# Attention on one core: halves of two key tiles weighed in pairs, and maxima moved within their turns

## The reference, cut to what matters

```python
h = gn(x)                                    # 32 groups of 16 channels
q, k, v = Wq h, Wk h, Wv h                   # 8 heads of 64 channels
attn = softmax(q^T k over the 2304 keys)     # no scaling
out  = x + gamma * (attn v) + Wsc h
```

## Time and profile before

| what | value |
| --- | --- |
| median of 3 runs | 3061.2 us (3058.46 to 3061.65) |
| time of the profiled execution | 3061.98 us |
| its span, first to last instruction | 3060.3 us |
| TensorE busy | 2967.9 us (97%) |
| GpSimd busy | 2765.5 us (90%) |
| VectorE busy | 2249.1 us (73%) |
| ScalarE busy | 1939.8 us (63%) |
| granted TensorE clock | 0.9 or more of full speed in each of the 40 slices, mean 0.997 |
| DMA | 112.71 MB, mean busy share below 0.2 of the engines after the first slice |

### The profile page before, as it was taken

The page is one execution under the profiler, slowest core; times in us unless marked ns, Lnnn a source line. Parts: engine busy times, 40 slices in busy tenths (PEclk is TensorE's granted clock), DMA queues, the critical chain, the costliest instruction groups (busy, mean ns, idle before and its releaser), DMA issues. The chain is left out here.

```text
span 3060.3 us, 149786 instructions
## 1 busy us (share of the span) xinstructions
PE 2967.9 (97%) x69035; PEld 2242.4 (73%) x69035; DVE 2249.1 (73%) x2856; ACT 1939.8 (63%) x3156; POOL 2765.5 (90%) x2039
## 2 busy tenths in 40 slices
PE   7999999999999999999999999999999999999998
PEld 4677777777777777777777777777777777777765
DVE  7777677777787767777777767777777777777774
ACT  4565676766566667676656567667666666666555
POOL 1798899999899999999989889999999989999898
PEclk9999999999999999999999999999999999999999
DMA  3111111111112011111011101111010101110101
GB/s 133 32 42 41 31 47 25 47 35 26 35 47 56 24 38 42 34 48 30 21 41 52 48 24 44 38 34 48 21 30 21 30 21 30 22 30 21 30 21 31
DMA packets 169076, 112.71 MB, mean 37 GB/s; under 512 B 120320, under 2 KB 166400, under 8 KB 168448
## 3 DMA queue, kind: packets, MB, share of 16 engines
q1 hardware_dynamic: 168448, 103.13, 12.8%
HBM read 56.10 MB, written 18.87 MB: 24 GB/s over the span
## 5 line engine op out<-in xcount | busy, mean ns | idle before, releaser
L984 POOL TENSOR_TENSOR PLO<-PE 128x768 f16<-128x768 f32 x1727 | 2531.7, 1479 | 226.0 <-ACT PE L613 203.5
L786 DVE TENSOR_REDUCE mx<-MX 128x2 f32<-128x768 f32 x1728 | 1654.6, 958 | 727.0 <-PE MX L444 705.2
L613 ACT ACTIVATE PE<-SL 128x768 f32<-128x768 f32 x1728 | 1400.4, 810 | 1020.2 <-PE SL L470 1020.1
L505 PE MATMUL OB<-V,PE 64*128 64x129 f16 x20736 | 1403.8, 219 | 1.2
L502 PE MATMUL OB<-V,PLO 64*128 64x65 f16 x20736 | 1307.1, 190 | 0.0
L505 PEld LDWEIGHTS OB<-V,PE 64*128 64x128 bf16 x20736 | 1034.4, 94 | 238.4 <-PE OB L502 82.9
L470 PE MATMUL SL<-QK 64*128 64x384 f16 x10368 | 1142.8, 324 | 11.7 <-ACT PE L613 6.5
L502 PEld LDWEIGHTS OB<-V,PLO 64*128 64x128 f16 x20736 | 968.9, 95 | 141.6 <-issue 0.2
L391 PE MATMUL PJ<-X,WT 64*128 64x384 f16 x6624 | 941.0, 323 | 0.0
L444 PE MATMUL MX<-QK 64*128 64x384 f16 x3456 | 579.4, 326 | 46.7 <-DVE mx L786 36.5
L470 PEld LDWEIGHTS SL<-QK 64*128 64x128 f16 x10368 | 440.6, 94 | 180.9 <-ACT PE L613 19.3
(11 more groups left out here) (108 smaller groups left out, 913.8 us busy)
## 6 DMA issues: line engine op xcount, KB each, us to landing
gx<-x SPq DMA_DIRECT2D x36, 768.0 KB, 4.7
xr<-x SPq DMA_DIRECT2D x96, 192.0 KB, 2.4
out<-xr SPq DMA_DIRECT2D x96, 192.0 KB, 1.9
X<-x SPq DMA_DIRECT2D x6, 768.0 KB, 8.5
CR<-c SPq DMA_TRANSPOSE x96, 2.3
back<-half SPq DMA_TRANSPOSE x95, 2.9
QK<-wk SPq DMA_DIRECT2D x1, 1024.0 KB, 12.7
QK<-wv SPq DMA_DIRECT2D x1, 1024.0 KB, 13.4
```

Of the source, the lines that this page charges most:

```text
L505: last = pe.matmul(acc, upper, v, start=begin, stop=False, skip_group_check=True)
L613: act.activation(PE32[:, s % PB, :].rearrange("p (h n) -> p h n", h=2), SL[:, :, 0:CH], ACT.Exp, scale=1.0 / SS).then_inc(s_exp, 1)
L786: nc.vector.tensor_reduce(mx3[:, n % 2, :, k], MX[:, :, 0:CH], AX.X, ALU.max).then_inc(s_mxf, 1)
L984: nc.gpsimd.tensor_tensor(PLO[:, s % PB, :], PE32[:, s % PB, :], PE32[:, s % PB, :].bitcast(BF16)[:, 1:4 * CH:2], ALU.subtract).then_inc(s ...
```

## The change

Four things are edited.

1. **Pairs.** In turns 0, 4, 9 and 13 TensorE weighs the first halves of two tiles, s - 3 and s - 2. In the turn after, it weighs the second half of s - 3 right behind `score` and the second half of s - 2 at the end. Both first halves use the same side and both second halves the other, so a pair has one swap. The side is now kept in a running variable. Tile s - 2 is weighed a turn sooner than before, and there are five buffers of exponentials and of their lower parts (`PB`).
2. **Turn 2** weighs the second half behind its first slot and no longer right behind `top`.
3. **Maxima.** In turns 6 and 11 (`EARLY`) `top` comes right behind `score`; in turns 8, 9 and 13 (`LATE`) it comes later: in 8 behind the slots, in 9 and 13 behind both first halves, ahead of the slots.
4. **VectorE.** The second addition moves from turn 10 to turn 11, and the statistics from turns 1, 5, 11 and 15 to 1, 2, 15 and 16.

```diff
@@ -24,7 +24,7 @@
 V1 = 2 * D + 1
 AW = D + 1
 OW = V1 + 1
-PB = 4
+PB = 5
 GROUP = C // 32
 EPS = 1e-5
 WS = 64.0
@@ -39,6 +39,8 @@
 TOPS = CHUNKS * MT
 LEAD = MT + 4
 LAG = 3
+EARLY = (6, 11)
+LATE = (8, 9, 13)
 
 
 KH, DH, DL, QH, QL = range(5)
@@ -251,9 +253,9 @@
 
         def stats_part(n, k):
             g, c = divmod(n, NCH)
-            if g % PAIRS or g // PAIRS + 1 == BATCH or k not in (1, 5, 11, 15):
+            if g % PAIRS or g // PAIRS + 1 == BATCH or k not in (1, 2, 15, 16):
                 return None
-            return (g // PAIRS, c, (1, 5, 11, 15).index(k))
+            return (g // PAIRS, c, (1, 2, 15, 16).index(k))
 
         def norm_piece(n):
 
@@ -471,6 +473,8 @@
                                          start=False, stop=a == DH and b == QL, skip_group_check=True)
                 last.then_inc(s_score, 1)
 
+            started, side = {}, [0]
+
             def weigh(s, part):
 
                 n, k = divmod(s, MT)
@@ -484,9 +488,11 @@
                         pe.wait_ge(s_rest, s + 1)
                     else:
                         pe.wait_ge(s_restd, 1)
-                else:
-                    pe.wait_ge(s_half, s + 1)
-                cross = (s + part) % 2
+                    started[s] = side[0]
+                elif side[0] == started[s]:
+                    pe.wait_ge(s_half, len(started))
+                    side[0] = 1 - side[0]
+                cross = side[0]
                 for i in range(QT):
                     for lower in range(2):
                         for half_rows in range(2):
@@ -555,15 +561,34 @@
                         slot(4 * n + b, lo + 2)
                         weigh(s - LAG, 1)
                         continue
-                    if s >= LAG:
-                        weigh(s - LAG, 0)
-                    if U < TOPS:
+                    if k in EARLY and U < TOPS:
                         top(U)
-                    if s >= LAG and (lo == 0 or k == 2):
-                        weigh(s - LAG, 1)
+                    if lo == 0:
+                        if s >= LAG:
+                            weigh(s - LAG, 0)
+                        if U < TOPS and k not in LATE:
+                            top(U)
+                        if s >= LAG:
+                            weigh(s - LAG + 1, 0)
+                        if U < TOPS and k in LATE:
+                            top(U)
+                    elif k - 1 in STARTS:
+                        if s > LAG:
+                            weigh(s - LAG - 1, 1)
+                        if U < TOPS:
+                            top(U)
+                    else:
+                        if s >= LAG:
+                            weigh(s - LAG, 0)
+                        if U < TOPS and k not in EARLY + LATE:
+                            top(U)
                     for i in range(lo, hi):
+                        if k == 2 and i == lo + 1 and s >= LAG:
+                            weigh(s - LAG, 1)
                         slot(4 * n + b, i)
-                    if s >= LAG and not (lo == 0 or k == 2):
+                    if U < TOPS and k in LATE and lo:
+                        top(U)
+                    if s > LAG and k != 2 and lo:
                         weigh(s - LAG, 1)
                     if root_unit(n, k):
                         root(*root_unit(n, k)[1:], U + 1)
@@ -940,8 +965,8 @@
                                 aggregate()
                     if k == 14 and n + 1 < CHUNKS:
                         shift_parts(n + 1)
-                    if k in (6, 10) and n >= 2:
-                        add_result(n - 2, (6, 10).index(k))
+                    if k in (6, 11) and n >= 2:
+                        add_result(n - 2, (6, 11).index(k))
                     if root_unit(n, k):
                         b, part = root_unit(n, k)[1:]
                         if part == 0:
```

## The result

The changed kernel takes 3043.0 us (median of 4 runs, 3041.3 to 3044.5) against 3059.8 us for the kernel before on the same chip (4 runs, 3058.2 to 3061.7). The ratio is 0.9944 with a 95% interval of 0.9932 to 0.9957. The forecast was 3046 us with a range of 3010 to 3076, so the direction and the size came out. The profiled execution took 3041.3 us with a span of 3039.6, against 3062.0 and 3060.3.

What follows compares the result with a forecast made beforehand. TensorE was taken as the bound (97% busy), GpSimd close behind (90%). Gains of 24.2 us in plain and 4.5 in normalizing chunks, less 13.5 for statistics, took 15.2 from 3061.2: 3046 us, range 3010 to 3076.

Steps and rivals of the forecast that it cites:

- Short swaps: TensorE, plain chunk: five swaps get covered by more work and save 0.07 us each, a gain of 0.35.
- Turns 8 and 12: Plain chunk: the maxima of these turns no longer wait for VectorE, gaining 0.36 and 0.29 us.
- Turn 6: Plain chunk: its early maximum must wait until turn 5's maximum has been read, a loss of 0.09 us.
- the slots of turns 9 (0.19) and 13 (0.35): Plain chunk: the first slot of each turn waits for VectorE's `leave`, losing 0.19 and 0.35 us.
- turn 3: Plain chunk: the new chunk's first half waits for the later evacuation, a loss of 0.06 us.
- Statistics: Later statistics delay the next image's load, so turn 3 stalls: 0.91 us in each of 15 chunks, 13.5 in all.
- Normalizing chunks: 18 chunks bound by GpSimd, needing 30.2 of 30.6 us: gain 0.25 each, 4.5 together, nothing if GpSimd is behind.
- A: Rival, slower: the additions on VectorE grow, so turns 8 and 13 pay 0.28 each; 3090 us, chance 0.12.
- B: Rival, faster: turn 11's addition gets ahead of GpSimd's split, so turn 13's slot loses nothing; 3019 us, chance 0.22.
- C: Rival, faster: none of the new waits comes; 2976 us, chance 0.04.
- D: Rival: a swap costs the same wherever it is, so pairs bring nothing; 3073 us, chance 0.06.

Runs made afterwards that it cites:

- pairs_only: The kernel before with only the pairs, the fifth buffer and turn 2's later second half; maxima, additions and statistics unmoved: 3043.4 us, ratio 0.9944.
- short_additions: The changed kernel with each of the two additions cut to 8 of its 384 columns: 3011.6 us, ratio 0.9841.
- stats_only: The kernel before with only the statistics moved, to turns 1, 2, 15 and 16: 3069.9 us, ratio 1.0034.
- change_old_stats: The changed kernel with the statistics back in turns 1, 5, 11 and 15: 3032.1 us, ratio 0.9910.
- addition_first: The kernel before, with GpSimd's split of turn 6 waiting for VectorE's first addition in chunks that do not normalize: 3014.9 us, ratio 0.9850.
- first_at_maximum: pairs_first_late_stats with GpSimd's split of turn 6 waiting for the maximum of turn 6, no longer for the addition's end: 2985.5 us, ratio 0.9759.
- moves_only: The kernel before with the maxima of turns 6, 8 and 11 and the second addition moved, no pairs, statistics as they were: 3047.3 us, ratio 0.9958.
- pairs_first_late_stats: pairs_only plus the GpSimd wait of addition_first, with the statistics in turns 4, 5, 10 and 15: 2998.3 us, ratio 0.9794.

## Why the prediction was right

**Short swaps (0.35 forecast).** Right. The swaps of turns 0, 2, 4, 9 and 13 are covered and 92 of 527 waits are left. By the medians of pairs_only the five gave 0.41, so 0.07 a swap was a little low.

**Turns 8 and 12 (0.36, 0.29).** Right. Their medians went from 1.92 to 1.57 and from 1.98 to 1.67.

**Turn 6 (0.09), the slots of turns 9 (0.19) and 13 (0.35), turn 3 (0.06).** Right. The medians of the turns are 1.76, 1.87, 2.02 and 1.81. From the starts above, the slots of chunk 21 were late by 0.18 and 0.30; in the median turn 13 is 0.35 longer than the 1.67 of three slots, its late maximum included. The forecast let the addition of turn 11 end 3.47 behind the start of its turn, as the one of turn 6 does; it does so in chunk 21, and short_additions shows why: its end hangs on the split.

**Statistics (13.5).** The mechanism was right, the size a little high. The load is issued 1.0 into turn 17, it lands 0.3 to 2.1 into turn 2, and turn 3 is longer. stats_only puts the cost at 10 us and change_old_stats at 11. The duration of the load was nearly right: I took 5.2 us for all 15 chunks, and in the changed kernel's trace these loads took 5.1 in the mean, nine of them less than 5. Turn 3 of the 15 chunks is 12.6 us longer there than at 1.81 each. The step that was too large is what this was set against. The forecast charged each stall against nothing, but the kernel before already had some: turn 3 took 2.25, 1.87 and 2.46 in chunks 4, 5 and 53, and 1.45 us more than 1.75 each over all 15. The difference is the 11 us of the experiments. VectorE waited for the load 9 times and not about 15: six loads landed 0.3 to 0.5 into turn 2, when VectorE had hardly come to need them. Turn 3 took 2.18 or 2.19 even there, so 0.37 of the cost is the statistics' place ahead of the maximum and the evacuation, and not the load.

**Normalizing chunks (4.5).** Too optimistic: they gave 1.0. The term that failed is GpSimd's need of 30.2 a chunk. It counted every split at 1.44, but the second addition, which has waited for one split, holds up the next for about 0.3 (1.78). With short additions, where this is gone, the chunks took 30.28, close to the 30.2 of the forecast; in the changed kernel they took 30.53. GpSimd was busy for 90.8 of 91.9 us there and TensorE had to wait for it. In the kernel before no weighing waited for a split; in the changed one

```profile
PEld OB L511 <- POOL PLO L1009: 11.5, 20, 0.8
```

and 17 of the 20 lie in turn 0, in normalizing chunks or behind them. This is the condition that the forecast named for a gain of nothing, the half a turn sooner that finds GpSimd behind. Turn 0 of the normalizing chunks is 0.24 longer than before; with short additions it is 0.07 longer.

**Rivals.** A (longer additions) did not decide; it appeared in small in pairs_only, as 0.07 in turn 12. B, the addition ahead of the split, did not happen by itself; GpSimd's split of turn 11 started ahead of the addition in all plain chunks, by 0.15 in the median, the distance that the forecast had worked out (1.6 and 1.75). But it was the right thing to look at: made to happen in turn 6 of the kernel before, it was worth 46 us. The rule cited there, that whichever of the two starts first keeps the other out for a whole instruction (the Trainium skill, SBUF — State Buffer, "SBUF: two separate sides"), agrees with both ways of setting the order, addition_first and first_at_maximum. C fell with the new waits of turns 9 and 13, in the changed kernel and in moves_only, and D with pairs_only.

That the total came out closer than its parts is luck: the gain missing in the normalizing chunks (3.5 us) was made up by the statistics (3.3 less than forecast), and these are two different errors.

## What to carry to other kernels

When a wait is moved away, work out at once what the instruction behind it will be late for: here three quarters of what turns 8 and 12 gave (0.65, of which moves_only kept 0.17) was taken again behind the same engine. An instruction that takes much longer than its own work, as the additions here with 1.46 to 1.73 us for 0.61, can be a wait in disguise; look whose end its end follows. Where two engines hold each other up, it paid here to order them by slack, and to let the one wait whose result is needed last.

## What the runs showed of the hardware that I had not expected

**The price of order between VectorE and GpSimd.** An addition of 384 columns takes 0.61 us when it comes first. When it comes second, it ends 0.41 behind GpSimd's running instruction, and takes up to 1.9 us in all. The split behind it is stretched in turn, from 1.47 up to 1.78. The `leave`s have the same width, but one of their two inputs lies in PSUM: 372 of them took 0.54 to 0.56 us, in the trace before and in the one after.

**A lower clock, by chance, behind a long wait.** Once for each image but the last TensorE waits 2.0 to 2.2 us for an exponential, in chunks 8, 32 and 56, while ScalarE loads tables twice (ACT_TABLE_LOAD, 1.28 us each). In the profiled execution of the kernel before, the granted clock behind that wait fell to half, 1.2 GHz, each of the three times; in that of the changed kernel never. Windows of chunk 8 behind the wait, the granted clock in the third column from the end, first the kernel before, then the changed one:

```profile
343.00:345.80 2.80, 2.80 (x38) 2.12 (x34) 1.50 (x3) 1.18 (x3) 2.51 (x3) 0.50 0.00 0
```

```profile
342.00:344.00 2.00, 2.00 (x54) 1.61 (x51) 2.00 (x4) 1.46 (x3) 2.00 (x2) 1.00 0.00 0
```

The price is seen within one kernel: in change_old_stats it came in chunk 32, which took 34.72, and not in chunks 8 and 56, which took 33.13 each, so 1.6 us a time and 4.8 between the two profiled executions. All ten kernels of the experiments show it behind this same wait, from once (pairs_only) to three times (pairs_first_late_stats); over all twelve profiled executions it came 19 times out of 36. What decides it from run to run stays open; no experiment was made on it.
